# Moving the last opening row's steps behind the first unit's products in a fused token model, attention and expert kernel

## What is computed

```python
def _L0_tok_ref(tokens, emb, W_upd, b_upd, W_f, b_f, decay_param, norm_g, norm_b, ...):
    mask = (tokens != 0).astype(emb.dtype)
    x = emb[tokens]
    x = x + _fast_memory(x, mask, W_upd, b_upd, W_f, b_f, decay_param)   # a scan over 512 steps
    x = _ln(x, norm_g, norm_b)
    for i in range(N_LAYERS):                       # 4 layers, 128 -> 512 -> 128
        h = _ln(x, cms_ln_g[i], cms_ln_b[i])
        h = jax.nn.gelu(jnp.einsum('bsd,df->bsf', h, cms_W1[i]) + cms_b1[i], approximate=False)
        h = jnp.einsum('bsf,fd->bsd', h, cms_W2[i]) + cms_b2[i]
        x = x + h
    return jnp.einsum('bsd,dv->bsv', x, head_W) + head_b
h = _L0_tok_ref(...)                                # 8 rows of 512 tokens
h = h + _L0_attn_ref(_layernorm(h, axis=-1), ...)
h = h + _L0_ffn_ref(_layernorm(h, axis=-1), ...)    # 8 experts, 2 chosen
return h
```

## Time and profile before

| what | value |
|---|---|
| device time, median of 3 runs | 427.89 us (425.44 to 429.58) |
| profiled execution, its own time | 426.03 us |
| its span | 424.2 us |
| mean granted clock of TensorE | 0.991 |
| TensorE, VectorE, ScalarE, GpSimd busy | 388.5, 351.3, 326.5, 269.2 us |

### The profile page before, as it was taken

The page is one execution under the profiler, slowest core; times in us unless marked ns, Lnnn a source line. Parts: engine busy times, 40 slices in busy tenths (PEclk is TensorE's granted clock), DMA queues, the critical chain, the costliest instruction groups (busy, mean ns, idle before and its releaser), DMA issues.

```text
span 424.2 us, 6301 instructions
## 1 busy us (share of the span) xinstructions
PE 388.5 (92%) x1977; PEld 312.4 (74%) x1977; DVE 351.3 (83%) x820; ACT 326.5 (77%) x558; POOL 269.2 (63%) x435
## 2 busy tenths in 40 slices
PE   4797879999999999999999989888887988999995
PEld 2586568888888888888888868677665756776883
DVE  3888689888898889888889889888777779989885
ACT  1254588999999998888977854667866989988994
POOL 0555787778777879778776556686434666435452
PEclk9699999999999999999999999999999999999999
DMA  6800011232212221222221000000000000000001
GB/s 211 338 2 0 1 24 29 50 51 51 40 35 51 50 53 26 50 51 50 37 39 50 2 0 2 1 2 2 0 0 2 0 2 13 12 15 12 14 13 25
DMA packets 15849, 14.94 MB, mean 35 GB/s; under 512 B 9796, under 2 KB 10568, under 8 KB 15560
## 3 DMA queue, kind: packets, MB, share of 16 engines
q1 hardware_dynamic: 15816, 14.54, 13.9%
HBM read 13.42 MB, written 1.11 MB: 34 GB/s over the span
## 4 chain that ended last, share of the span: by engine, by line
PE 63%; DVE 17%; ACT 13%; issue 4%; POOL 2%; DMA 1%; SPq 0%; DVEq 0%; ACTq 0%
PE ps L1439 56%; PE ps L1462 4%; ACT hid L869 4%; ACT w_all L875 3%; ACT ezf L804 2%; DVE hid L1381 2%; DVE hh L1232 1%; DVE stats L949 1%; PE ps L1470 1%; DMA xn<-in_w_f 1%; DVE x L1381 1%; ACT scratch L865 1%; ACT scratch L769 1%; ACT hid_lo L825 1%; DVE xn_lo L1388 1%
## 5 line engine op out<-in xcount | busy, mean ns | idle before, releaser
L683 ACT ACTIVATE hid<-ps,b_fold 128x512 f32<-128x512 f32 x128 | 84.0, 681 | 21.2 <-PE ps L1439 20.8
L1023 DVE TENSOR_TENSOR hid_lo<-hid,hid_hi 128x1024 fp32r<-128x1024 f32 x64 | 78.6, 1228 | 25.4 <-ACT hid_hi L688 25.2
L1439 PE MATMUL ps<-xn_hi,w_all 128*128 128x512 f32 x256 | 87.5, 403 | 0.6 <-DVE xn_lo L1018 0.6
L1439 PE MATMUL ps<-hid_hi,w_all 128*128 128x512 f32 x256 | 85.0, 393 | 0.0
L688 ACT ACTIVATE hid_hi<-hid 128x1024 fp32r<-128x1024 f32 x64 | 67.9, 1061 | 2.0
L1439 PEld LDWEIGHTS ps<-xn_hi,w_all 128*128 128x128 f32 x256 | 48.4, 189 | 10.8 <-issue 0.9
L1439 PEld LDWEIGHTS ps<-hid_hi,w_all 128*128 128x128 f32 x256 | 48.1, 188 | 9.9
L1439 PE MATMUL ps<-xn_lo,w_all 128*128 128x512 f32 x128 | 49.9, 390 | 0.0
L1439 PE MATMUL ps<-hid_lo,w_all 128*128 128x512 f32 x128 | 49.8, 389 | 0.0
L869 ACT ACTIVATE hid<-ps,eb_fold 128x512 f32<-128x512 f32 x64 | 44.1, 688 | 0.2
L1439 PE MATMUL ps<-hid_hi,ew 128*128 128x512 f32 x128 | 41.8, 409 | 1.1 <-ACT hid L869 0.8
(11 more groups left out here) (229 smaller groups left out, 895.6 us busy)
## 6 DMA issues: line engine op xcount, KB each, us to landing
rstd_row<-roots SPq DMA_DIRECT2D x29, 256.0 KB, 4.1
hh<-in_tokens SPq DMA_DIRECT2D x8, 256.0 KB, 7.8
hid<-in_w SPq DMA_DIRECT2D x1, 1024.0 KB, 7.1
rstd_row<-in_w SPq DMA_DIRECT2D x1, 1024.0 KB, 10.2
out<-hh SPq DMA_DIRECT2D x7, 128.0 KB, 2.0
ew_raw<-in_expert_w SPq DMA_DIRECT2D x1, 512.0 KB, 9.9
roots<-rstd SPq DMA_DIRECT2D x29, 2.0 KB, 1.4
ew_raw<-in_expert_w SPq DMA_DIRECT2D x1, 256.0 KB, 10.0
```

The source lines that it names most:

```text
L683: act.activation(hid[:, j % 2, f, :], bank[f], ACT.Gelu, bias=b1_fold[:, j // B * F + f:j // B * F + f + 1]).then_inc(gelu_done, 1)
L1023: dve.tensor_tensor(hid_lo[:, j % 2, 2 * p:2 * p + 2, :], hid[:, j % 2, 2 * p:2 * p + 2, :], hid_hi[:, j % 2, 2 * p:2 * p + 2, :].bitcast( ...
L1439: return pe.matmul(out, lhsT, rhs, start=start, stop=stop)
```

## The change

In front of unit 0's products:

- GpSimd takes the one-hot matrix of row 7 from VectorE, behind its first pair.
- TensorE gets 12 more spare products: six behind the first look-ups, and three each behind the second norm's turns of units 0 and 1.
- The `broadcast`s of rows 0, 1, 3 and 4 stand earlier, in front of bias products, spare products or a turn.
- VectorE no longer does row 7's scan in the opening loop. Behind the loop it does `norm(4)`, `w1_lo(0)` and `norm_x(0)`, and then `scan(7)`, the bias additions and `x_lo(0)`.

Behind unit 0's products: TensorE's `centre_w1(1)`, the spread of row 5 (place 6) and the turns of places 9 and 10; on VectorE the statistics of row 6 (place 8), `pre(7)`, `norm(5)` and the statistics of places 9 and 10, all behind `x_lo(0)`; on ScalarE `w1_hi(1)`, behind the first Gelu; `w1_lo(1)` behind `norm_x(1)`.

```diff
-POOL_ROWS = (3, 4, 5)
+POOL_ROWS = (3, 4, 5, 7)
...
             inverse_root_of_pair(0)
+            one_hot(POOL_ROWS[3])
             inverse_root_of_pair(2)
...
-            w1_hi(1)
             affine(4)
...
+                    if f == 0 and j == 0:
+                        w1_hi(1)
...
-            for n in range(B):
+            for n in range(B - 1):
                 scan(n)
...
-                if n in (6, 7):
-                    norm(2 * n - 10)
+                if n == 6:
+                    norm(2)
...
-            w1_lo(0)
...
+            norm(4)
+            w1_lo(0)
             norm_x(0)
+            scan(7)
+            folds_added()
+            x_lo(0)
+            row_stats(place_in(6) % 4, place_in(6) + 1)
+            pre(7)
+            norm(5)
             row_stats(place_ffn(2) % 4, place_ffn(2) + 1)
-            x_lo(0)
-            norm(5)
             row_stats(place_in(7) % 4, place_in(7) + 1)
-            w1_lo(1)
             for j in range(L * B):
...
+                if j == 0:
+                    w1_lo(1)
...
             look_up(1)
+            keep_clock_at(0, bank[5])
+            keep_clock_at(0, bank[5])
             for n in range(1, B):
                 turn(x[:, n - 1, :], pre_ready, n, place_in(n - 1))
                 look_up_embedding(n)
-                if n in (6, 7):
-                    broadcast(place_in(2 * n - 10) % 4, place_in(2 * n - 10))
+                if n == 6:
+                    broadcast(2, 2)
                 if n + 1 < B:
                     look_up(n + 1)
+                if n in (4, 5):
+                    broadcast(n - 4, n - 4)
...
+                if n == 6:
+                    broadcast(3, 3)
...
-                if n in (4, 5, 6):
-                    broadcast((0, 1, 3)[n - 4], (0, 1, 3)[n - 4])
...
-                if n >= 5:
+                if n in (5, 6):
                     turn(x[:, n - 5, :], x0_ready, n - 4, place_ffn(n - 5))
-            centre_w1(1)
-            broadcast(place_in(5) % 4, place_in(5))
-            turn(x[:, B - 1, :], pre_ready, B, place_in(B - 1))
+                    keep_clock_at(n, bank[5])
+                if n == 6:
+                    broadcast(place_in(4) % 4, place_in(4))
             keep_clock_at(B - 1, bank[2])
             pe.wait_ge(w1_lo_ready, 1)
...
                 up(j)
+                if j == 0:
+                    centre_w1(1)
+                    broadcast(place_in(5) % 4, place_in(5))
+                    turn(x[:, 2, :], x0_ready, 3, place_ffn(2))
+                    turn(x[:, B - 1, :], pre_ready, B, place_in(B - 1))
```

More of the change, by code:

```diff
@@ L503, in _ @@
             pool.wait_ge(onehot_dve, POOL_ROWS[0])
-            for n in POOL_ROWS:
+            for n in POOL_ROWS[0:3]:
                 one_hot(n)
@@ L987, in _ @@
                     one_hot(2)
-                if n in (2, 3):
-                    one_hot(n + 4)
-                if n in (6, 7):
-                    norm(2 * n - 10)
+                if n == 2:
+                    one_hot(6)
+                if n == 6:
+                    norm(2)
                 if n >= 1:
@@ L994, in _ @@
                 pre(n)
[L995 to L1001, removed]
                 if n in (4, 5, 6):
@@ L1005, in _, with folds_added @@
                     row_stats(place_ffn(n - 5) % 4, place_ffn(n - 5) + 1)
-            w1_lo(0)
+            def folds_added():
+                dve.wait_ge(folds_done, 1)
+                dve.tensor_tensor(eb1_fold[:, :], bank[5][:, L * F:L * F + E], cols[:, C_EB1:C_EB1 + E], ALU.add)
+                dve.tensor_tensor(br_fold[:, :], bank[5][:, L * F + E:L * F + 2 * E], rows[:, R_BR:R_BR + E], ALU.add)
+                dve.tensor_tensor(b1_fold[:, :], bank[5][:, 0:L * F], cols[:, C_B1:C_B1 + L * F],
+                                  ALU.add).then_inc(folds_ready, 1)
             def norm_x(j):
@@ L1478, in look_up @@
                 else:
-                    pe.wait_ge(onehot_dve, 1 + n - len(POOL_ROWS) * (n > POOL_ROWS[0]))
+                    pe.wait_ge(onehot_dve, sum(k not in POOL_ROWS for k in range(n + 1)))
                 if n >= 2:
```

## The result

The changed kernel takes 430.94 us in the median of 15 runs (428.59 to 433.26), the kernel before 426.34 us (425.36 to 430.76, also 15). The ratio is 1.0086 with a 95% interval of 1.0061 to 1.0112: slower by 3.7 us, clear of noise and under 1% (the two medians lie 4.6 us apart). The forecast was +2.4 us, on a base of 427.89 that turned out 1.5 us high. Executions more than 1.5% above the fastest of the same version are left out of every ratio; these are three, all of one version, given at the end.

A forecast was written before the change was run, and what follows sets the result against it. TensorE was taken to bound the kernel, so only the start of up(3) counted. Terms -2.95 + 4.55 + 0.8 + 0 = +2.4 us on the median 427.89 gave 430.3 us, range 426.2 to 433.4.

The forecast's parts named there:

- Term 1: TensorE's opening: up(0) starts 2.95 us earlier, at 44.0 instead of 46.95.
- Term 2: Behind up(0): the chain from row 5's spread through statistics and GpSimd's roots to norm(6) and up(1) grows by 4.55 us.
- Term 3: GpSimd's queue to place 11's root, then store and load: unit 3's root comes later still, +0.8 us.
- Term 4: TensorE's granted clock, opening and new gap before up(0): effects taken to cancel, 0 us (-0.8 to +2.8).
- the prediction's own sign of being wrong: TensorE's clock: a reading below 1.00 from 41 to 50 us, or shorter waits behind up(0), would show it wrong.
- The reading against it, 252 to 256 us: Later TensorE stretch: busy only 1.95 of 4.00 us yet clock 1.00, taken as evidence against a fall before up(0).
- the sum was near +4.5: TensorE's new gap: if transposes do not protect the clock, the total would be near +4.5 us, not +2.4.
- the rival in which the clock falls: Clock falls before up(0): +2.4 us and 1.8 to 2.8 more, 432.1 to 433.1 us; chance 0.13.
- Edits at nothing: Opening: row 7's one-hot on GpSimd, earlier spreads and spare products at units 0 and 1; spreads expected under 0.2 us.
- the lead is kept: Behind up(0): statistics and GpSimd's pair hide under TensorE's work, only moved work counts, -0.8 us, 427.1 us; chance 0.17.
- `norm_x(0)` is less free: Opening: norm_x(0) waits for norm(4), up(0) leads by only 1.95 us, sum +3.4, 431.3 us; chance 0.05.
- the forecast's case: Start of up(3) in the layers: later by 1.6 to 4.0 us; chance 0.60.

The follow-up runs named there:

- the gap filled: The changed kernel with nine more spare products in TensorE's gap before unit 0's products: ratio 1.0076 to the kernel before, median 430.04 us.
- the front part: The kernel before with only row 7's one-hot on GpSimd, 12 spare products and earlier spreads of rows 0, 1 and 3: ratio 0.9984.
- The repaired version: The changed kernel with row 5's spread and centre_w1(1) before unit 0's products, place 9's turn inside, w1_hi(1) before the first Gelu, w2_lo later: ratio 0.9982.
- the part behind: The changed kernel's moves behind unit 0's products; run alone, without the front edits and row 4's earlier spread: ratio 1.0132 to the kernel before.

## Why the prediction was right, and where its sizes were off

**What bounds the kernel.** The question was when `up(3)` starts, and that held for the order's effect. It left out that the clock in the later stages differs from execution to execution; 1.6 of the 6.2 us between the two profiled executions lie there. Of the 4.6 us by which the changed kernel's `up(3)` is later, counted from the first look-up, 2.2 are left with the gap filled and the clock held (59.90 against 57.69). That is near the forecast's +2.4; the rest is the clock.

**Term 1** was right in mechanism and size: 2.95 forecast, 3.03 measured, with `up(0)` at 43.92 for 44.0.

**Term 2**, the growth of the chain behind `up(0)`, was forecast at 4.55 us. With the clock held it is 12.78 less 8.22, 4.56. Its links stood near where they were put: VectorE idle before `norm(5)` for 3.03 us in that trace, and the root of place 8 9.9 us after the start of `up(0)` (43.31 to 53.22), as in the working (44.0 to 53.9). But the working hangs everything on row 5's spread, and there the runs say more. With the spread alone ahead of the products, 13.76 us from `up(0)` to `up(1)` less 1.57 for the slow clock leaves 12.2, hardly less than 12.78. With `centre_w1(1)` ahead too it is 11.33, and with the turn of place 9 inside the products 10.07. The turn stood behind the same products: with the gap filled it ended at 48.05, 0.2 us before `norm(5)` let the statistics start, so the spread and the turn both had to move. From the statistics of place 9 two branches then lead to the spread of place 8, the root on GpSimd and TensorE's own queue (the turn of place 10, `norm_x(1)`, `w1_lo(1)`, `centre_w1(3)`). They end level, at 53.22 and 53.27 us with the gap filled, as the working also had them; which of the two bounds is not shown.

**Term 3**, GpSimd's queue, place 11, store and load, was forecast at 0.8. With the clock held it costs 0.45 in the order of the change (6.40 less 5.96); the load landed 23.93 us after `up(0)` started, for 24.2 in the working (where the terms for place 11's root add up to 62.4 and not 62.2). The section of the Trainium skill named there (DMA: Bandwidth & Descriptors, "Anatomy of one DMA") describes transfers issued by GpSimd, and these are issued by SyncE: with the gap filled the store took 2.63 us and the load 3.05. In the profiled execution of the changed kernel it costs nothing, for `up(2)` was so late by then that the load had landed in time.

**Term 4**, the clock, is the step of the sum that was mis-sized: taken at 0, with bounds of -0.8 and +2.8. In the changed kernel's profiled execution it is +3.2: 1.60 us in `up(0)` and 1.61 more between `up(1)` and `up(2)` (9.54 against 7.93 before), less than 0.5 of which term 3 gives back. The gap of 2.51 us before `up(0)`, named as the danger, was followed by the fall, and a clock below 1.00 between 41 and 50 us was the prediction's own sign of being wrong. A second fall, behind the wait of 57.79, was not foreseen. The other traces bear the first out: the clock fell in `up(0)` behind waits of 2.51, 2.53 and 2.15 us, and also behind one of 1.21 us with a spread in front of it; it stayed where the place was filled with nine spare products or with `centre_w1(1)`.

The reading against it, 252 to 256 us, was chance and was read wrongly. It was taken from one execution, and TensorE's wait there stands in every version. The kernel before, the same place with the gap filled, and the clock behind it in that trace:

```profile
254.16 1.17 PE L1439 MATMUL ps<-wqkv,xn_hi 128*128 128x256 f32 x8 [2.05 <-ACT rstd_row L781]
```

```profile
255.56 1.54 PE L1448 MATMUL ps<-wqkv,xn_hi 128*128 128x256 f32 x8 [2.05 <-ACT rstd_row L783]
```

```profile
256.00:260.00 4.00, 4.00 (x24) 3.85 (x22) 3.77 (x14) 0.22 (x1) 2.77 (x5) 0.57 0.01 4
```

In eight of the twelve traces of the table the clock fell within 1.3 us of the end of this wait, in four it did not. Nor is the work from 252 to 256 us much of it transposes: all 17 products of that row are ordinary ones (the weights `wqkv` and `headw`), so it is no evidence on transposes. By the Trainium skill, TensorE: Matmul & The Clock Gate, "Part 4: PE-mode transpose", the sum was near +4.5; the profile came out at +4.7 by `up(3)`. The sums agree, but no run here tells transposes from other products, so the rule itself is not shown.

Over all executions the clock term is smaller than in the profiled one: the ratio gives 3.7 us where the two profiles differ by 6.2. How much of the 3.7 is clock can't be read from mean clocks. The kernel before has 0.991 in its profile although it read 1.00 from 25 to 420 us; its one long fall lies at 10 to 25 us, and holding the clock over 14 to 22 brought no time. The changed kernel has no fall there in its profile; its lower clock lies elsewhere, and in the layers a fall cost 1.6 us. At 0.992 it took 428.59, 429.00 and 429.68 us, and the kernel before at 0.991 or 0.992 took 426.57 in the median of 21 executions beside the experiments. These 2.4 us equal the forecast's, but that is no proof of the forecast's order.

**Luck.** The forecast of 430.3 us lies 0.6 from the measured 430.94 only because its base was 1.5 us high. On 426.34 it gives 428.7, and the rival in which the clock falls, which had a chance of 0.13, gives 430.5 to 431.5.

**Edits at nothing.** Row 7's one-hot on GpSimd, the spare products and the spreads of rows 0, 1 and 3 moved nothing together (35.90 against 35.58 us to `up(0)`), so "under 0.2" stands for those. With row 4's spread among them the front part carries 2 of the 3 us of lead, and the wait of `norm(4)` points to that spread.

**The rivals.** That the lead is kept did not happen. The repaired version keeps 0.7 us of it at `up(3)`, when row 5's spread, `centre_w1(1)` and the turn of place 9 are not queued behind the products and GpSimd's split is out of the way. That `norm_x(0)` is less free did not happen: it started at 40.79. The clock rival, as it was written (the forecast's case and a fall before `up(0)`), did happen in the profiled execution; of the others only the times are known.

**Left open:** what makes the clock fall behind a wait in one execution and not in another. The later falls may have to do with the opening or not: behind the wait of 2.05 us the clock fell in eight of the nine traces that have the part behind, and in none of the three without it, though the code is the same there; with one trace each this is a hint. No version beats the kernel before by more than the interval of its ratio.

## What to carry to other kernels

Steps that head a chain over several engines (here a spread and a turn that release statistics, and behind them a root on GpSimd and the next norm) must not be queued behind a long block of products just because their results are not wanted at once: count the whole chain back from the next place where it is wanted. If two such steps stand behind the block, moving one brings little, as the spread alone did. Work moved out of the way of a start belongs first into the gap that the earlier start opens; here it cost nothing there and kept TensorE busy as well. And a gain of 1 us in one stage is lost to the eye when executions differ by 4 us through the clock. Compare the lengths of stages, and look where in each trace the clock fell: the mean clock does not say whether a fall cost time.

## What the hardware showed that I had not expected

The same wait of TensorE, 2.05 us in the same code, was followed by a fall of the granted clock to 0.50 in eight traces and by none in four. A fall in the layers cost 1.6 us (`up(0)` 4.42 instead of 2.82 us); the one at 14 us cost almost nothing, since VectorE was the slower there. One and the same kernel, that with the gap filled, ran at a mean granted clock of 0.980 to 0.996 and took 427.7 to 433.6 us.

The version with the spread and `centre_w1(1)` ahead had one execution that was granted 0.75 over 100 to 300 us, neither of the two usual levels, and took 494.32 us. Another took 646.89 us at a mean of 0.56, and a third 436.56 us at 0.972.
